# Where the first register loads stand among TensorE's dummy transposes, and how many of these there are

## The reference, cut to what matters

```python
# x (64, 64, 1024), condition (64,) int in 0..15, weights (16, 64, 64)
y = einsum('bct,bcd->bdt', x, weights[condition])      # one 64x64 matrix per b, chosen by index
base = einsum('bth,oh->bto', y, W_up)                   # 1024 -> 1024
top1 = argmax(y_flat @ gate_w.T + expert_bias)          # 4 experts
z = einsum('nh,erh->ner', y_flat, lora_A)               # rank 8
delta = einsum('ner,ehr->neh', z, lora_B) * 1.0, of the expert top1 alone
out = x + base + delta
```

## Time and profile before

| | |
|---|---|
| median of 3 runs | 445.52 us (444.39 to 446.64) |
| profiled execution, its own time | 445.25 us |
| its span, first to last instruction | 443.4 us |
| PE busy | 433.8 us (98%) |
| DVE, ACT, POOL busy | 351.4, 198.3, 116.7 us |
| dummy transposes, line 638 | 62, 9.6 us |
| first real matmul | at 12.07 us of the span |

### The profile page before, as it was taken

The page is one execution under the profiler, slowest core; times in us unless marked ns, Lnnn a source line. Parts: engine busy times, 40 slices in busy tenths (PEclk is TensorE's granted clock), DMA queues, the critical chain, the costliest instruction groups (busy, mean ns, idle before and its releaser), DMA issues.

```text
span 443.4 us, 8927 instructions
## 1 busy us (share of the span) xinstructions
PE 433.8 (98%) x3138; PEld 411.3 (93%) x3139; DVE 351.4 (79%) x643; ACT 198.3 (45%) x310; POOL 116.7 (26%) x95
## 2 busy tenths in 40 slices
PE   8899998999999999999999999999999999999996
PEld 8789997999999999999999999999999999999995
DVE  3899879698796969789686969879696978969653
ACT  4895436253544426244543625354352624454210
POOL 3992040130505022050504013050503204050400
PEclk9999999999999999999999999999999999999999
DMA  9900032130412122140313113041212214032102
GB/s 216 406 21 1 2 120 71 54 139 24 148 41 104 61 89 100 47 142 24 118 56 109 71 51 138 24 139 50 98 67 94 95 47 142 24 118 70 50 30 90
DMA packets 17231, 38.73 MB, mean 87 GB/s; under 512 B 3838, under 2 KB 3838, under 8 KB 17218
## 3 DMA queue, kind: packets, MB, share of 16 engines
q1 hardware_dynamic: 16018, 38.02, 24.3%
q10 hardware_dynamic: 1040, 0.26, 0.3%
q0 software_dynamic: 160, 0.28, 0.3%
HBM read 21.78 MB, written 16.78 MB: 87 GB/s over the span
## 4 chain that ended last, share of the span: by engine, by line
PE 82%; DVE 6%; issue 6%; POOL 2%; DMA 2%; ACT 0%; DVEq 0%; POOLq 0%
PE bank_y L598 25%; PE bank_x L598 24%; PE y_ps L534 11%; PE bank_c L598 10%; PE bank_b L598 9%; DMA lora_b_sb<-in_L_ffn_lora_B_dram 2%; DVE w_s L780 1%; DVE w_a L780 1%; DVE x_hl L747 1%; PE bank_y L604 1%; PE bank_c L604 1%; PE bank_x L604 1%; PE bank_b L604 1%; POOL lora_b L305 1%; DVE hl_s L757 1%
## 5 line engine op out<-in xcount | busy, mean ns | idle before, releaser
L310 POOL TENSOR_TENSOR s_sum<-a 128x512 f32<-128x512 f32 x16 | 20.7, 1293 | 294.7 <-DVE a L752 294.7
L368 ACT ACTIVATE x_hl<-x_sb 64x1024 fp32r<-64x1024 f32 x64 | 67.8, 1059 | 58.9 <-DMA x_sb<-in_x_dram 58.1
L747 DVE TENSOR_TENSOR x_hl<-x_sb,x_hl 64x1024 fp32r<-64x1024 f32 x64 | 78.2, 1221 | 9.1 <-ACT x_hl L368 7.2
L598 PE MATMUL bank_x<-w_a,hl_a 128*128 128x292 f32 (+1 forms) x576 | 76.1, 288 | 0.0
L598 PE MATMUL bank_y<-w_a,hl_a 128*128 128x292 f32 (+1 forms) x576 | 76.0, 288 | 0.0
L598 PEld LDWEIGHTS bank_y<-w_a,hl_a 128*128 128x128 f32 x576 | 73.6, 189 | 0.5
L598 PEld LDWEIGHTS bank_x<-w_a,hl_a 128*128 128x128 f32 x576 | 73.5, 189 | 0.5
L372 ACT ACTIVATE y_small<-y_ps 128x512 f32<-128x512 f32 x62 | 37.1, 599 | 74.1 <-PE y_ps L534 74.1
L534 PE MATMUL y_ps<-cond_hl,x_hl 128*128 x496 | 63.8, 272 | 2.5 <-DVE a L752 1.0
L534 PEld LDWEIGHTS y_ps<-cond_hl,x_hl 128*128 128x128 f32 x496 | 61.5, 191 | 5.0 <-DVE a L752 1.4
L752 DVE TENSOR_TENSOR a<-y_ps,y_small 128x512 f32<-128x512 f32 x62 | 42.6, 686 | 13.0 <-ACT y_small L372 12.4
(11 more groups left out here) (126 smaller groups left out, 476.5 us busy)
## 6 DMA issues: line engine op xcount, KB each, us to landing
x_sb<-in_x_dram SPq DMA_DIRECT2D x32, 512.0 KB, 3.4
out_dram<-x_sb SPq DMA_DIRECT2D x64, 256.0 KB, 2.0
w_raw<-in_L_ffn_W_up_dram SPq DMA_DIRECT2D x8, 512.0 KB, 11.7
cond_sb<-in_L_cond_weights_dram ACTq DMA_DIRECT2D x1, 256.0 KB, 5.5
cond_sb<-in_L_cond_weights_dram SPq DMA_DIRECT2D x1, 256.0 KB, 6.6
router_sb<-in_L_ffn_lora_A_dram POOLq DMA_DIRECT2D x1, 128.0 KB, 8.1
lora_b_sb<-in_L_ffn_lora_B_dram POOLq DMA_DIRECT2D x1, 128.0 KB, 8.4
router_sb<-in_L_ffn_gate_w_dram POOLq DMA_DIRECT2D x1, 16.0 KB, 6.1
```

The source lines that it names most:

```text
L310: pool.tensor_tensor(s1_sum[:, :], a21[:, :], a22[:, :], ALU.add).then_inc(s1_added, 1)
L368: act.activation(x_hl[rows, t, b, :], x_sb[rows, 2 * par + t, :], ACT.Copy).then_inc(x_high, 1)
L598: mm = pe.matmul(dst, hl[op][:, a, k, :], w[:, b, k, cols], start=(fresh and k == 0 and a + b == 0), stop=(k == KH - 1 and a == 1), skip_g ...
L747: dve.tensor_tensor(x_hl[other, t, b, :], x_sb[rows, 2 * par + t, :], x_hl[rows, t, b, :].bitcast(fp32), ALU.subtract).then_inc(x_low, 1)
```

## The change

62 transposes in one group become 24, then the wait for the index list and the four register loads, then 22 more, 46 in all. Nothing else changes. The transposes write the same bank as before.

```diff
-    WARM_UP = 62
+    WARM_UP = (24, 22)
...
             pe.wait_ge(ident_done, 1)
-            for _ in range(WARM_UP):
-                pe.transpose(bank_x[:, 0, 0:P], ident[:, :], ident[:, :])
+            def warm_up(n):
+                for _ in range(n):
+                    pe.transpose(bank_x[:, 0, 0:P], ident[:, :], ident[:, :])
+
+            warm_up(WARM_UP[0])
             pe.wait_ge(index_loaded, 16)
             index = [load_index(0, t) for t in range(2)]
+            warm_up(WARM_UP[1])
             pe.wait_ge(cond_low, 1)
             make_y(0, 0, 0, index[0], FIRST_Y[0][0])
```

## The result

| | before | after |
|---|---|---|
| median of 18 runs each | 445.08 us | 447.01 us (446.05 to 448.21) |
| ratio, 95% interval | | 1.0045 (1.0036 to 1.0053) |
| profiled execution, its span | 445.25, 443.4 us | 448.06, 446.3 us |

The change costs 1.9 us, 0.45%. That is clear of noise, and under the 0.5% that the prediction took as the bound for "slower". The runs shown ahead of the prediction were three; beside the changed kernel the median of before is 445.08.

The account below looks back on a forecast made before the run. PE, busy 98%, was taken to bound the kernel, so only the first real matmul's start could move: 2.1 us late less 0.3 slack gives 1.8, and 445.25 + 1.8 = 447.0 us; 8-in-10 range 445.0 to 448.5.

Parts of the forecast that it names:

- When the list lands: Index list's DMA, third on SP's queue: taken to land at 7.8 us, within bounds of 4.75 and 9.0.
- the early rival (c): Index list lands early, by 4.75 at best; loads run beside the first group: 445.1 us, chance 0.15.
- The pause: PE between the two transpose groups: nothing to do from 6.8 to 10.6 us, 3.8 us, until the loads end.
- The second group: 22 transposes from 10.6 us: 3.6 us, between 2.4 and 4.8, starting at 1.2 GHz; first make_y at 14.2, 2.1 late.
- rival (b): Second group and into make_y: clock stays at 1.2 GHz, 4.2 us at most, 448.3 to 449.4 us; chance 0.13.
- Rival (a): Second group: clock kept through the pause, 2.4 us, make_y at 13.0, 0.7 us remain, 445.9 us; chance 0.22.
- How far the delay carries: From make_y to the loop: 2.1 us late less 0.3 slack at piece 0 of s2, 1.8 us, nothing given back after.
- rival (d): DVE and POOL give back 0.5 us or more of the delay: 446.3 us; lower part of the forecast's joint 0.50.
- The sum: Whole kernel: 445.25 + 1.8 = 447.0 us; by the median shown, a cost of 1.5 us or 0.3%.
- No gain from 16 transposes fewer: Dummy transposes at the start: the 16 dropped would have run in the pause, so no work leaves the path.
- three signs of being wrong: First load before 5 us; make_y before 12.1; or make_y 2 us late with the loop starting on time.

Follow-up runs that it names:

- the count alone: The changed kernel with WARM_UP = (46, 0), all 46 dummy transposes in one group ahead of the register loads: 445.48 us, ratio 1.000 to the kernel before.
- (42, 22): The changed kernel with 42 dummy transposes in place of 24 ahead of the loads, then 22: 445.49 us, ratio 1.0010 to the kernel before.
- (24, 0): The changed kernel without its second group, so 24 dummy transposes, the loads, then make_y: 446.55 us, ratio 1.0040 to the kernel before.

## Why the prediction was right, step by step

- **When the list lands: right.** 7.8 was taken from the transfer that stands ahead of it; the trace shows 7.70. In the other kernels with the list third on SP's queue whose first load was not held up by transposes, that load ran at 7.3 to 8.0. The early rival (c) did not happen.
- **The pause: right in kind, 0.6 us short.** 3.8 us from 6.8 to 10.6 was forecast; it was 4.42 from 6.15 to 10.57. The loads took 2.87, where 2.8 was taken. The first group ended sooner since the clock rose at 5.2 in this execution and not at 6.9.
- **The second group: right as a range, low for the profiled execution.** 3.6 us was taken between 2.4 and 4.8; the profile shows 4.6, near the upper end, which is rival (b)'s. But the timed runs lie in two groups 1.1 us apart, neither at the end where the clock is kept. Taken off the profiled start (3.11 us late), the 1.1 us put the faster group's start at about 2.0 late, an estimate, where 2.1 was forecast. Rival (a), 445.9, falls: every run had a mean clock of 0.996 or less. What (b) priced on top, `make_y` itself at half clock, did not come: it took 1.21 us.
- **How far the delay carries: the term that was mis-sized.** 0.26 was to come off, since DVE is busy 4.97 of every 5 us and passes on everything. 0.74 came off by block 0 (3.11 to 2.37). 0.35 of it came off by s2, where 0.26 was taken; the rows already had DVE idle for 0.43 behind it, ahead of 19.05. The rest came off at one DVE subtraction that takes 1.19 us in the kernel before and 0.74 after. So a busy share of 99% was read as work throughout, while part of it goes with POOL's work beside it. Then the loop of the profiled pair added 0.46 again. At the end 0.28 is missing from the 3.11, near the 0.26 by two errors that cancel. That is rival (d) at block 0, in size about as it had it, and not at the end.
- **The sum: 1.8 us forecast, 1.9 measured, in part by luck.** The 1.9 lies between two groups of runs, 1.6 and 2.7 us above the median of before, and the profiled pair differ by 2.8. The middle that was taken for the second group, for want of a row, fell near the faster and larger group. The forecast's way of carrying the delay was wrong by 0.5 us at block 0 and right at the end.
- **No gain from 16 transposes fewer: right**, by the count alone (1.000).
- **The signs.** None of the three signs of being wrong was seen: the first load ran at 7.7, `make_y` started at 15.18, and the loop started late. Two details missed in the profiled execution: no transpose of the second group took 273 ns, and piece 0 of s2 started at 20.52 in place of 19.6.

## What to carry to other kernels

A wait moves to the front of whatever is queued behind it: before moving one up, find the time at which its data lands, not the time at which the old place stopped waiting. Up to block 0 the dummy transposes and the clock mattered here through the time at which real work got done: (46, 0) and (42, 22) cost nothing that clears the noise, the first even in runs whose clock fell, and (24, 22) cost 0.45%. A start in time is no warrant for the total: (24, 0) was 0.2 us late at block 0 and lost 0.40% by the end, and where the loop lost it is not shown. An engine that is busy 99% of the time may still give a delay back, where part of an instruction's time goes with another engine's work beside it; compare single durations before and after, not only idle times.

## What the runs showed that was not expected

- A DMA issued 0.55 us later (ACT's half of the matrices) landed 9 us later. Why is not shown.
- Eight dummy transposes more on TensorE (72 against 64), ahead of everything, go with a stall before 72 us: 72 transposes or more cost 1.0 to 1.6 us there, as the time from block 0 to block 1 rose from 20.4 to between 21.3 and 22.0 in all five profiles with 72 or more.
- The clock that fell in a pause of 4.4 us stayed at 1.2 GHz until 15.4, 4.8 us after the transposes had begun again.
- The clock also fell after a pause was over, with TensorE at work: with 46 in one group at 12.2, 1.2 us after `make_y` had begun behind a pause of 2.41 us, and with the list first on SP's queue at 13.5, 2.3 us after `make_y` had begun behind a pause of 1.93.
